# A two-layer graph network on one core: the first microseconds reordered, two tiles scaled one by one, and constant matmuls in front

## The reference, cut to what matters

```python
def layernorm(x): return (x - mean(x)) / sqrt(var(x) + 1e-5)      # over the 1024 features

# x: 1250 nodes x 1024; src, dst: 20000 edges, sorted by dst; w: one weight for each edge
h  = relu(layernorm(x))
s  = sigmoid(h @ wenc.T + benc)                                   # 1250 x 500
agg = segment_sum((s @ wconv)[src] * w[:, None], dst)
x  = x + (agg + s @ wlin.T) @ wdec.T + bdec
h  = relu(layernorm(x))
x  = x + normalised_adjacency(src, dst) @ (h @ W.T + b)           # second layer, with self loops
```

## Time and profile before

| | |
|---|---|
| median of 3 runs | 506.05 us (505.86 to 507.28) |
| the profiled execution: its own time | 507.28 us |
| its span on the core | 505.2 us |
| PE busy in the span | 485.8 us, 96% |
| DVE busy | 258.7 us, 51% |
| ACT busy | 172.9 us, 34% |
| POOL busy | 34.3 us, 7% |

### The profile page before, as it was taken

One profiled execution on the slowest core, in us unless ns is written; L12 is line 12 of the kernel. 1 busy time (PEld: TensorE's weight loads), 2 busy tenths in 40 slices (PEclk: granted clock), 3 DMA queues, 4 the chain that ended last, 5 costly groups with the idle time before them and its releaser, 6 DMA issues.

```text
span 505.2 us, 9376 instructions
## 1 busy us (share of the span) xinstructions
PE 485.8 (96%) x3696; PEld 417.5 (83%) x3696; DVE 258.7 (51%) x552; ACT 172.9 (34%) x342; POOL 34.3 (7%) x34
## 2 busy tenths in 40 slices
PE   2889999999999999999999999999999999999997
PEld 1889999978887787789888878888888888888884
DVE  7878896787856874534468787511211111211211
ACT  2846874745541141124245546500200110120200
POOL 5100000000000000000000000120030030030030
PEclk9999999999999999999999998999999999999999
DMA  8520124382110230064610008011011001001002
GB/s 315 211 75 22 56 69 135 89 320 84 63 53 0 74 130 2 4 265 167 244 38 0 2 10 325 1 42 43 1 43 42 3 6 77 3 0 68 18 7 71
DMA packets 16479, 40.12 MB, mean 79 GB/s; under 512 B 2000, under 2 KB 10458, under 8 KB 16050
## 3 DMA queue, kind: packets, MB, share of 16 engines
q1 hardware_dynamic: 16114, 39.08, 21.2%
q0 software_dynamic: 320, 0.39, 0.3%
HBM read 27.94 MB, written 11.52 MB: 78 GB/s over the span
## 4 chain that ended last, share of the span: by engine, by line
PE 87%; DVE 7%; ACT 4%; issue 1%; DMA 0%; POOL 0%; ACTq 0%; DVEq 0%; POOLq 0%
PE bank L1086 21%; PE bank L1087 20%; PE bank L1088 20%; PE bank L1102 17%; PE bank L1192 2%; DVE stats L785 1%; PE bank L1212 1%; PE bank L1307 1%; PE bank L1194 1%; PE bank L1196 1%; ACT h L633 1%; ACT we L648 1%; DVE h0T L885 1%; DVE o_key L878 1%; DVE before L805 1%
## 5 line engine op out<-in xcount | busy, mean ns | idle before, releaser
L1102 PE MATMUL bank<-a,h_hi 128*128 128x256 f16 (+3 forms) x400 | 87.5, 273 | 0.0
L1102 PE MATMUL bank<-a,h_lo 128*128 128x256 f16 (+3 forms) x400 | 87.4, 272 | 0.0
L1086 PE MATMUL bank<-w_hi,z 128*128 128x512 f32 (+1 forms) x160 | 62.7, 392 | 1.1 <-DVE z L1061 1.1
L1071 DVE SCALAR_TENSOR_TENSOR x<-bank,dis_u,x 128x512 f32<-128x512 f32 (+1 forms) x20 | 14.9, 750 | 95.3 <-PE bank L1088 95.3
L1087 PE MATMUL bank<-w_lo,z 128*128 128x512 f32 (+1 forms) x160 | 62.4, 390 | 0.0
L1088 PE MATMUL bank<-w_hi,z 128*128 128x512 f32 (+1 forms) x160 | 62.3, 389 | 0.0
L756 ACT CAST z<-bank 128x256 fp32r<-128x256 f32 (+1 forms) x40 | 14.4, 371 | 129.1 <-PE bank L1102 129.1
L621 POOL TENSOR_TENSOR x<-x,bt 128x1024 f32<-128x1024 f32 (+1 forms) x10 | 24.0, 2397 | 396.4 <-ACT bt L764 396.4
L1086 PE MATMUL bank<-h0T,we 128*128 128x256 f32 (+3 forms) x160 | 47.0, 294 | 3.3 <-DVE hT L892 2.0
L1061 DVE TENSOR_TENSOR z<-bank,z 128x256 fp32r<-128x256 f32 (+1 forms) x40 | 16.4, 417 | 57.0 <-ACT z L756 56.8
L1087 PE MATMUL bank<-h0T,we 128*128 128x256 f32 (+3 forms) x160 | 45.5, 284 | 0.0
(11 more groups left out here) (146 smaller groups left out, 1030.2 us busy)
## 6 DMA issues: line engine op xcount, KB each, us to landing
adj_scratch<-stage SPq DMA_DIRECT2D x50, 125.0 KB, 1.8
raw<-adj_scratch SPq DMA_DIRECT2D x2, 2500.0 KB, 10.0
h<-x SPq DMA_DIRECT2D x9, 512.0 KB, 5.4
x<-x SPq DMA_DIRECT2D x9, 512.0 KB, 5.2
out<-x SPq DMA_DIRECT2D x9, 512.0 KB
w_raw<-w SPq DMA_DIRECT2D x4, 1024.0 KB, 9.3
wd_raw<-wdec SPq DMA_DIRECT2D x1, 2048.0 KB, 8.2
we_raw<-wenc SPq DMA_DIRECT2D x2, 1000.0 KB, 9.3
```

The costliest lines, as they stand in the source:

```text
L1071: v.scalar_tensor_tensor(xs, bank[banks_of[g]][0:n, :], dis_u[0:n, t:t + 1], xs, ALU.mult, ALU.add).then_inc(bank_free, 1)
L1086: pe.matmul(o, lhs[0], rhs[0], start=first, stop=False, skip_group_check=True)
L1102: ins = pe.matmul(o, h1[i][0:n, k, 128 * f:128 * (f + 1)], moving, start=(k == 0 and part == 0 and i == 0), stop=(k == T - 1 and part == p ...
```

## The change

The step list begins otherwise. The comparisons become a step of their own and are split in two halves of five. The statistics of tile 0 are followed at once by its scaling, then by tile 1's (before, one scaling served both). The twenty matmuls of the search (`find`) move behind the transposes of block 0. The step `starts` moves behind the remainders of all four banks of block 0, and the statistics of tile 3 and the joint scaling of tiles 2 and 3 move behind `starts`. PE begins with 36 matmuls on constant tables, 250 columns each, whose result nobody reads.

```diff
--- before.py
+++ after.py
@@ -51,6 +51,7 @@
 AHEAD = 2
 OPEN = 4.0
 PAIR = 2
+FILL = 36
 HSCALE = 1024.0
 MAGIC = 12582912.0
 EPS = 1e-5
@@ -103,9 +104,10 @@
     t0 = turn(0)
     lo = [("lo", *s) for s in t0]
 
-    steps = statistics(0)[:3] + [("starts",), ("idents",)] + statistics(0)[3:] + norms(0) + statistics(1)[:3] + cut_we[:1]
-    steps += t0[:1] + statistics(1)[3:] + cut_we[1:2] + t0[1:2] + lo[:2] + cut_we[2:3] + t0[2:] + cut_we[3:4] + lo[2:]
-    steps += cut_we[4:6] + norms(1)[:1] + cut_we[6:] + norms(1)[1:] + [("parts",)]
+    steps = [("before", 0), ("stats", 0), ("var", 0, 1), ("stats", 1), ("scale", 0, 1), ("norm", 0), ("var", 1, 2), ("before", 1)]
+    steps += [("scale", 1, 2), ("norm", 1), ("idents",), ("stats", 2)] + cut_we[:1] + t0[:1] + cut_we[1:2] + t0[1:2] + lo[:2]
+    steps += t0[2:] + [("find",)] + cut_we[2:3] + lo[2:] + [("starts",), ("stats", 3), ("var", 2, 4)] + cut_we[3:5] + statistics(1)[3:]
+    steps += cut_we[5:6] + norms(1)[:1] + cut_we[6:] + norms(1)[1:] + [("parts",)]
     dense = encoder(0)[:PAIR] + [("fields",)] + turn(1) + statistics(2) + norms(2) + encoder(0)[PAIR:] + [("edges",)]
 
     for b in range(1, NB):
@@ -235,6 +237,9 @@
                 accs[g] = len(accs)
                 if s[0] in ("t", "g", "s", "z"):
                     his[g] = len(his)
+
+    calls = [s for s in STEPS if s[0] == "var"]
+    scaled = {t: i + 1 for i, (_, a, b) in enumerate(calls) for t in range(a, b)}
     cuts = {s: i for i, s in enumerate([s for s in STEPS if s[0] == "cut"])}
 
     with ExitStack() as ctx:
@@ -598,7 +603,7 @@
                                                      bass.IndirectOffsetOnAxis(ap=start[:, j:j + 1], axis=0)).then_inc(rows_in, 16)
                 elif s[0] == "var":
                     t0, t1 = s[1:]
-                    pool.wait_ge(var_ready, t0 // 2 + 1)
+                    pool.wait_ge(var_ready, scaled[t0])
                     nc.gpsimd.tensor_tensor(std[:, t0:t1], dis[:, t0:t1], minus_half[:, 0:t1 - t0], ALU.pow).then_inc(power_ready, 1)
                 elif s[0] == "general":
                     pool.wait_ge(missed_ready, 1)
@@ -629,7 +634,7 @@
                 if s[0] == "norm":
                     t = s[1]
                     n = tile_rows(t)
-                    act.wait_ge(rstd_ready, t // 2 + 1)
+                    act.wait_ge(rstd_ready, scaled[t])
                     nc.scalar.activation(h0[t % XRING][0:n, :], h0[t % XRING][0:n, :], ACT.Relu, bias=nbias[0:n, t:t + 1],
                                          scale=rstd[0:n, t:t + 1]).then_inc(relu_ready, 1)
                 elif s[0] == "roots1":
@@ -742,7 +747,7 @@
                 elif s[0] == "norm1":
                     t = s[1]
                     n = tile_rows(t)
-                    act.wait_ge(rstd_ready, T // 2 + t + 1)
+                    act.wait_ge(rstd_ready, len(calls) + t + 1)
                     nc.scalar.activation(h1[0][0:n, t, :], x1[t][0:n, :], ACT.Relu, bias=nbias[0:n, t:t + 1],
                                          scale=rstd[0:n, t:t + 1]).then_inc(h1_hi_ready, 1)
                     if t >= 2:
@@ -801,11 +806,12 @@
             dve.wait_ge(iotas, 4)
             dve.wait_ge(heads_in, 16)
             link(v.tensor_copy(heads[:], heads_i[:]))
-            for c in range(HC):
-                ins = v.tensor_scalar(before[:, c, :], firsts[:], heads[:, c:c + 1], None, ALU.is_gt)
-            ins.then_inc(before_ready, 1)
             for s in STEPS:
-                if s[0] == "stats":
+                if s[0] == "before":
+
+                    for c in range(HC // 2 * s[1], HC // 2 * (s[1] + 1)):
+                        v.tensor_scalar(before[:, c, :], firsts[:], heads[:, c:c + 1], None, ALU.is_gt).then_inc(before_ready, 1)
+                elif s[0] == "stats":
                     t = s[1]
                     n = tile_rows(t)
                     dve.wait_ge(x_in[t], 16)
@@ -827,7 +833,7 @@
 
                     t0, t1 = s[1:]
                     y, q, var = std[:, t0:t1], dsq[:, t0:t1], dis[:, t0:t1]
-                    dve.wait_ge(power_ready, t0 // 2 + 1)
+                    dve.wait_ge(power_ready, scaled[t0])
                     link(v.scalar_tensor_tensor(q, y, -0.5, y, ALU.mult, ALU.mult))
                     link(v.tensor_tensor(q, q, var, ALU.mult))
                     link(v.scalar_tensor_tensor(rstd[:, t0:t1], q, 1.5, y, ALU.add, ALU.mult))
@@ -1161,15 +1167,19 @@
 
 
             pe.wait_ge(iotas, 11)
-            pe.wait_ge(before_ready, 1)
-            for j in range(RG):
-                for c in range(HC):
-                    ins = pe.matmul(wbank[1][0:EP, 2 * ROWS + 2 + j:2 * ROWS + 3 + j], before[:, c, EP * j:EP * (j + 1)], ones16[0:EP, :],
-                                    start=(j == 0 and c == 0), stop=(c == HC - 1), skip_group_check=True)
-            ins.then_inc(starts_acc, 1)
+            for i in range(FILL):
+                pe.matmul(bank[XBANKS - 1][:, 0:WC], iota_s[:], iota_k[:], start=(i == 0), stop=(i == FILL - 1), skip_group_check=True)
 
             for s in STEPS:
-                if s[0] == "edges":
+                if s[0] == "find":
+
+                    pe.wait_ge(before_ready, HC)
+                    for j in range(RG):
+                        for c in range(HC):
+                            ins = pe.matmul(wbank[1][0:EP, 2 * ROWS + 2 + j:2 * ROWS + 3 + j], before[:, c, EP * j:EP * (j + 1)],
+                                            ones16[0:EP, :], start=(j == 0 and c == 0), stop=(c == HC - 1), skip_group_check=True)
+                    ins.then_inc(starts_acc, 1)
+                elif s[0] == "edges":
 
                     pe.wait_ge(fields_ready, 1)
                     for i, (o, c) in enumerate(((wbank[0], 0), (wbank[0], ROWS), (wbank[1], 0), (wbank[1], ROWS), (take(s), 0))):
```

## The result

The change made the kernel slower: 510.77 us median of 6 runs (509.61 to 511.11) against 506.75 us (505.86 to 507.86, 6 runs), a ratio of 1.0073 (95% interval 1.0054 to 1.0092). The forecast was 509.7 us, which is 1.0072 of the 506.05 us that were known. The profiled execution took 511.11 us with a span of 508.8 us, 3.6 us more than before.

A forecast was written before the change was run, and what follows sets the result against it. PE bounds from 28.30 us; ACT getting through its list up to `parts` sets that start. Head 0, constants 0, late power and scaling +3.64, landing 0: +3.6 us on the 506.05 median, 509.7 us; whole range 508.2 to 512.0.

The forecast's parts named there:

- The head: Start of the kernel up to the first bank's copy on ACT: at 12.55 instead of 14.80, won by 2.2 us.
- 0 for the head: Term of the sum: the 2.2 us won at the start count nothing, lying before a wait that ends later.
- the 3.64: Term for the late power and scaling of tiles 2 and 3: relu of tile 2 at 22.9 instead of 19.26.
- The constants and the search, nothing: PE's 36 constant matmuls end between 6.6 and 10.2, under a wait; the moved search adds nothing at `parts`.
- Row numbers, gathers: DVE and POOL: row numbers done at 17.8 instead of 9.6, first gather at 18.0, POOL free at 20.95.
- The power of tiles 2 and 3: On POOL behind the gathers, from 20.95, taken as 1.08 us, not 0.71, so done at 22.05.
- the rule alone: Shared-port rule for POOL's power of tiles 2 and 3: DVE waiting, power 0.71 us, delay 3.3 us.
- The landing, nothing: Gathers of `edges`: second lands by 27.0 at latest, 0.8 us after ACT asks; bounds 0 to 0.8, taken as nothing.
- the second rival: Gather landing holds at 7.3 us in an emptier queue and `parts` waits: +0.8, 510.5 us; chance 0.13.
- PE ahead of the restart: First two feature groups end at about 26.5, block 1's transposes at 28.4; PE then waits over 3 us before 31.9.
- the first rival: PE's clock falls in the idle gap, slowing encoder groups behind 31.9: +0.7 to +2.3 more, 510.4 to 512.0; chance 0.25.
- The third rival: Faster: the 2.2 us lead lives if `parts` starts before 22.56, giving 503.8 us; chance 0.05.

The follow-up runs named there:

- Late starts alone: Kernel before, with only the row numbers, tile 3's statistics and the scaling of tiles 2 and 3 moved to the late place; ratio 1.0117 to before.
- Early: Changed kernel with the search ahead of the transposes, and row numbers, tile 3's statistics and the power right behind it; ratio 0.9998 to the kernel before.
- later loads: "Early" with SP waiting for the gathers to land before issuing the loads of tiles 6 and 7; 505.77 us against 507.22 before, ratio 0.9975.
- power first: Changed kernel with tile 3's statistics and the power of tiles 2 and 3 ahead of the row numbers and gathers; ratio 1.0112 to the kernel before.
- memsets later: "later loads" with POOL's two big memsets moved behind the powers of tiles 0 and 1; ratio 1.0000 to the kernel before.
- before with constants: Kernel before, with 16 constant matmuls added behind its search; ratio 0.9994 to the kernel before.
- no constants: Changed kernel without its 36 constant matmuls; 509.61 us median, ratio 1.0058 to the kernel before.

## Why the prediction was right, and which terms were off

The mechanism is as put: a gain at the head, and a scaling of tiles 2 and 3 that is late because the row numbers are, and because POOL's power stands behind the gathers. The terms that were off are small here, and some cancel. The steps, with what they measured:

- **The head.** Forecast: first relu 8.7, second 10.8, first bank's copy 12.55. Measured 9.04, 10.75 and 12.52. The term that was mis-sized is the five comparisons ahead of tile 0: 1.33 us forecast as half of ten in the earlier trace rows, 1.69 measured (3.50 to 5.19). The ten are not equal, as the view of line 813 shows (min/median/max ns, first and last start):

```profile
L813 DVE TENSOR_SCALAR before<-firsts,heads x10: 269/282/1127, 3.5 to 9.8; 125x250 f16<-125x250 f16 x10
```

  The one of 1127 ns is the first, at 3.50, and ends 0.08 us after POOL's second memset (4.55); this wait stays whole in the first half. It made the relu of tile 0 late, but not that of tile 1, which lets the banks begin: the second half was shorter by as much (9.00 to 9.97), and the ten together took 2.66 us as in the earlier trace rows.
- **"0 for the head".** The sum reads as if the head were worth nothing. In its own working the row numbers' time (17.8) counts from the earlier relu of tile 1, so 2.2 us of gain were inside the 3.64. "Late starts alone" shows it: 5.8 us of loss without the head, 3.4 with it.
- **The constants and the search, nothing.** The constants ended at about 9.0, inside the bounds of 6.6 to 10.2 and ahead of the end of the relu of tile 0 (10.28); without them the restart was 0.33 us later. The search took 1.27 us and ended before the encoder's first input was ready (idle 0.74 before 14.98).
- **Row numbers, gathers.** Row numbers done at 17.76 for 17.8, first gather at 18.09 for 18.0, POOL free at 21.15 for 20.95.
- **The power of tiles 2 and 3.** I took 1.08; it was 0.74. The page "SBUF — State Buffer" of the Trainium skill, in "Who interferes with whom", says that a DVE instruction with two inputs in SBUF contends with a GpSimd instruction that reads SBUF. By that rule the longer time belongs to what DVE ran beside the power, and it was right where I took the row nearest in place: DVE stood idle for 1.28 us until 21.93, all through the power. With DVE's start 21.93 the relu came at 22.71 for 22.9, and the delay at the restart was 3.44 for 3.64; the rule alone gave 3.3.
- **The landing, nothing.** 5.2 us at most instead of 7.3, so the second rival was out. "Early" and "later loads" show that the 7.3 of the earlier trace rows was no constant of the gather; it was 8.9 us with two tile loads issued between the pair and 5.0 without.
- **PE ahead of the restart.** Forecast: feature groups done at 26.5, transposes at 28.4, then over 3 us idle. Measured: about 28.0, 30.1, and 1.64 us. This sign was wrong, without effect on the time. Slices 5 to 7 came in time, but from 25.31 PE ran at the lower level (1.2 GHz; clock 0.50 in 26 to 28 us), 0.21 us a matmul, after three waits of 1.42, 1.55 and 0.95 us. At 0.12 us its twelve matmuls would have ended near 26.7 (an estimate), as forecast. So the clock fell ahead of the restart, where it was hidden, and had risen again by 31.74, behind a gap of 1.64 us. That this is why the first rival did not happen here is my reading of the rows, not tested. Where the gap was long it did: 1.1 us in "power first" after 5.87 us, within its 0.7 to 2.3, and 0.3 us in "early" after 3.90 us, below it. The 3 us that it put before slice 3 were 1.42 us, as PE had spent 0.21 us on most of the matmuls before.
- **The third rival's margin.** It says that gathers that cost POOL nothing would miss by 0.7 us. By the prediction's own lower bound (power at 19.45, behind DVE's addition) only 1.5 us can be saved there, so the miss would be 2.1 us. The rival was further off than written.

## What to carry to other kernels

A step that issues work on several engines has a place in each engine's list: before moving it later, ask on each of them what then stands behind it, here the power of the next tiles behind two gathers. The first link of a long chain (search, row numbers, gather, copies, fields) can move behind work that is needed sooner only by as much as the chain has slack; here about 3 us. `parts` already was what PE's restart waited for, but it waited for ACT's list: in the kernel before the gathers had landed by 19.5 for `parts` at 22.56, and the bias of tiles 2 and 3 was ready at 16.1 for a relu at 19.26. The row numbers moved by 8.2 us (9.44 to 17.59). And a transfer that ends a chain is best kept clear of loads that nobody needs yet: one wait on SP's queue turned an order that gained nothing into the fastest, by 0.25% under the kernel before.

## What the runs showed of the hardware

**POOL's memsets hold some of DVE's instructions whole.** In the kernel after, DVE's cast of 10 columns:

```profile
2.30 1.13 POOL L594 MEMSET hT<- 32x1250 f32 x1
2.38 1.09 DVE L808 CAST heads<-heads_i 125x10 f32<-125x10 int32 x1 [0.78 <-DMA heads_i<-heads_dst]
3.38 1.17 POOL L595 MEMSET hT<- 32x1250 f32 x1
```

With the memsets later, the same instruction and the comparisons behind it:

```profile
2.50 0.17 DVE L811 CAST heads<-heads_i 125x10 f32<-125x10 int32 x1 [0.89 <-DMA heads_i<-heads_dst]
2.70 1.07 DVE L816 TENSOR_SCALAR before<-firsts,heads 125x250 f16<-125x250 f16 x5
```

The cast ends at 3.47 with the first memset (3.43), not after its own 0.17 us; so it did in nine of the ten traces that have the memsets at this place, beginning 0.04 to 0.24 us behind the first. In the tenth, "before with constants", it began 0.16 us behind and took 2.08 us, across both; why it then let the second memset go first is not shown. The page "SBUF — State Buffer" of the Trainium skill, in "Who interferes with whom", says of casts and `tensor_scalar` in their two-port mode that whichever engine comes first holds the shared pair for its whole instruction and the other blocks; these rows agree, with the memset first each time.

**The power took longer beside DVE's line 457 (452).** 1.08 us for 128x2 in the earlier trace rows and in "before with constants", 0.18 us behind the start of one; 0.86 in the two early orders without constants, where it overlapped the end of one; 0.70 to 0.74 elsewhere in the first 40 us, but for one of 0.79 in "late starts alone", which began while DVE formed the identities (lines 820 and 821). Spans on POOL are rough.

**The time to the landing of the same gather** was 4.9 to 5.2 us for the slower of the pair in the seven traces in which no tile load was issued while it was under way (in "power first" one was, 0.1 us before the landing). In the four others it was 8.9 us with two of them begun between the pair ("early"), and 6.9, 7.2 and 7.3 us with two begun 1.1, 2.4 and 3.9 us behind its own issue. Only "early" and "later loads" differ by the loads alone; in the rest other things differ too.

**A step of about 1.6 us between executions of one kernel.** Some profiled executions have a stretch at the lower clock at the start of the second layer, as the one before in the earlier trace rows, and take 203.9 to 204.1 us from there to the end (seven of the eleven traces, clock 0.51 to 0.61 in the 3.5 us behind the first 3); the others have none and take 202.4 or 202.5 (no constants: 304.86 to 507.3). The times of the kernel before lie in two groups to match: of 35 runs beside "early, later loads", 11 took 505.56 to 506.31 us and 24 took 506.96 to 507.96. That the stretch follows the matmuls of two columns is in the rows; why one execution has it and the next not stays open. The start of the second layer leaves this out, and is for this reason the better measure of what an edit in the first 30 us is worth, though of one execution only.
